# Second feed-forward of a two-layer block: down projection in fp32r halves, with the weight stationary

## The reference

```
def _L1_ffn_ref(x, Wr, Wg, Wu, Wd, Sg, Su, Sd):      # E, K, F = 16, 2, 64; FS = 128
    shared = silu(xf @ Sg) * (xf @ Su) @ Sd
    probs = softmax(xf @ Wr)
    topk_p, topk_i = top_k(probs, K)
    cw = zeros((T, 16)).at[arange(T)[:, None], topk_i].add(topk_p)
    for e in range(16):
        routed += (silu(xf @ Wg[e]) * (xf @ Wu[e]) @ Wd[e]) * cw[:, e:e+1]
    return routed + shared
```

## Time and profile before

| | |
|---|---|
| median of 3 runs | 1448.84 us (1448.66 to 1451.96) |
| the profiled execution | 1449.45 us, its span 1447.5 us |
| PE / PEld busy | 1299.0 / 988.7 us (90% / 68%) |
| DVE busy | 1126.0 us (78%) |
| ACT / POOL busy | 971.2 / 757.9 us (67% / 52%) |
| the second feed-forward | from about 1236 us to the end, some 211 us |
| its PE L2256 (down) | 576 matmuls and as many weight loads |

### The profile page before, as it was taken

How to read it: one execution, slowest core, us unless ns; L and a number is a source line. 1 busy time by engine, 2 the same in 40 slices (tenths; PEclk the granted TensorE clock), 3 DMA queues, 4 the chain that set the end, 5 groups by cost and what they waited for, 6 DMA issues and landing times. The chain is left out here.

```text
span 1447.5 us, 34194 instructions
## 1 busy us (share of the span) xinstructions
PE 1299.0 (90%) x12121; PEld 988.7 (68%) x12121; DVE 1126.0 (78%) x3042; ACT 971.2 (67%) x1499; POOL 757.9 (52%) x972
## 2 busy tenths in 40 slices
PE   2799999999999689999928999999999998799997
PEld 1466666666655377888816777777777776688886
DVE  5578888888877566999856888888888776476776
ACT  1688888888887357777724777777777877344441
POOL 4775675787763364899765454556444330101112
PEclk9899999999999779999957999999999999899999
DMA  6000000111111030222122111111111110225253
GB/s 237 18 22 22 20 22 21 25 30 34 29 31 40 8 89 28 60 74 74 56 84 55 49 48 48 47 48 47 49 47 38 40 41 19 58 61 128 71 132 82
DMA packets 84429, 77.20 MB, mean 53 GB/s; under 512 B 18224, under 2 KB 72240, under 8 KB 83888
## 3 DMA queue, kind: packets, MB, share of 16 engines
q1 hardware_dynamic: 80176, 66.73, 17.4%
q0 software_dynamic: 4096, 8.40, 2.0%
HBM read 36.26 MB, written 13.63 MB: 34 GB/s over the span
## 5 line engine op out<-in xcount | busy, mean ns | idle before, releaser
L541 ACT ACTIVATE a_p<-a_ps_s 128x1024 f32<-128x1024 f32 x256 | 258.4, 1031 | 21.6 <-PE a_ps_s L400 21.2
L1313 DVE TENSOR_REDUCE a_qt<-a_ps_d 128x2 fp32r<-128x512 f32 x256 | 174.9, 690 | 42.8 <-PE a_ps_d L1092 37.3
L651 DVE TENSOR_REDUCE a_qt<-a_ps_d 128x2 fp32r<-128x512 f32 x256 | 174.6, 688 | 40.1 <-PE a_ps_d L411 38.4
L822 POOL TENSOR_TENSOR a_rn<-a_ss,a_half 128x16 f32<-128x16 f32 x56 | 162.6, 2921 | 1.3
L1214 ACT ACTIVATE a_pg<-a_ps_s 128x1024 f32<-128x1024 f32 x128 | 125.8, 1024 | 24.0 <-PE a_ps_s L1081 22.4
L1092 PE MATMUL a_ps_d<-a_kpad,a_qs 128*128 128x512 f32 x256 | 126.4, 497 | 4.2 <-DVE a_qt L1313 1.5
L418 PE MATMUL a_ps_o<-a_p,a_v 128*32 128x256 f32 x2048 | 126.9, 387 | 3.7 <-ACT a_p L541 3.7
L411 PE MATMUL a_ps_d<-a_kpad,a_qs 128*128 128x512 f32 x256 | 126.2, 494 | 3.0 <-DVE a_qt L651 2.6
L2335 ACT ACTIVATE f_s<-f_ps_g 128x512 f32<-128x512 f32 x72 | 43.0, 598 | 99.5 <-PE f_ps_g L2271 99.3
L1501 POOL DMA_INDIRECT a_picked<-ys,rows x64 | 67.5, 1054 | 61.5 <-PE a_ps_d L1092 50.7
L418 PEld LDWEIGHTS a_ps_o<-a_p,a_v 128*32 128x32 f32 x2048 | 60.4, 110 | 51.3 <-issue 19.4
(11 more groups left out here) (370 smaller groups left out, 3829.7 us busy)
## 6 DMA issues: line engine op xcount, KB each, us to landing
a_kpad<-a_kc SPq DMA_DIRECT2D x512, 32.0 KB
f_gb<-spread SPq DMA_DIRECT2D x64, 256.0 KB, 5.6
a_kpad<-a_kq SPq DMA_DIRECT2D x256, 32.0 KB, 1.8
f_xin<-xs SPq DMA_DIRECT2D x39, 128.0 KB, 2.1
ys<-f_yout SPq DMA_DIRECT2D x39, 128.0 KB, 2.1
w<-in_w SPq DMA_DIRECT2D x2, 2304.0 KB, 11.5
out_x<-X SPq DMA_DIRECT2D x8, 256.0 KB, 6.6
xs<-f_zero SPq DMA_DIRECT2D x15, 128.0 KB, 1.9
```

The lines of the kernel that those rows point to most:

```text
L541: nc.scalar.activation(probs[:, u % 2, 2 * c:2 * c + 2, :, :].rearrange("p a b c -> p (a b c)"), ps_s[:, 2 * c:2 * c + 2, :].rearrange("p ...
L651: nc.vector.tensor_reduce(qt2[:, (k - PEAK) % 4, 2 * part:2 * part + 2, SHIFT], bank(k, f"m{part}")[:, :].rearrange("p (a b) -> p a b", b= ...
L822: nc.gpsimd.tensor_tensor(rn[:, part * c:(part + 1) * c], ss[:, part * c:(part + 1) * c], half[:, 0:c], ALU.pow).then_inc(rn_ready, 1)
L1313: nc.vector.tensor_reduce(qt[:, b % 2, GLOBAL, n:n + 2, SHIFT], bank(k, f"m{part}")[:, :].rearrange("p (j s) -> p j s", s=S), AX.X, ALU.ma ...
```

## The change

The down projection is done in fp32r halves, as the up projection already is. Per piece there are now three matmuls of 512 columns (weight high with product high, weight low with product high, weight high with product low), and the weight's halves wdh and wdl are stationary, so that the sum in ps_y has features on the partitions. The halves of the product are made anew for every piece: ACT casts it to ph (`high`), and POOL (q = 0, 2, 4, 6, 7, 8) or DVE (q = 1, 3, 5) subtracts ph from it into pl (`low`). ph and pl have three buffers each. The finished sum is copied to yb by ACT and turned back by four TensorE transposes into a new PSUM tile ps_b, from which DVE now takes statistics (at q = 3 and 4, before q = 1 and 2) and the normalisation. A piece of p is free when its pl is written (before: when `down` was done), and h[0] is free when pl of piece 0 is written. wdh and wdl are made once, in step 0.

```diff
+    BY_VECTOR = (1, 3, 5)
+    BY_POOL = tuple(q for q in range(NQ) if q not in BY_VECTOR)
+    TURN_BACK = 2
...
+        acc, yb = sb("acc", [P, TOK]), sb("yb", [P, TOK])
+        ph, pl = sb("ph", [P, 3, TOK], F32R), sb("pl", [P, 3, TOK], F32R)
+        wdh, wdl = sb("wdh", [P, NQ * D], F32R), sb("wdl", [P, NQ * D], F32R)
+        ps_b = pb("ps_b", [P, TOK])
...
@@ PE, down(st, q, block)
-                for t in range(TT):
-                    src = h[:, 0, t * P:(t + 1) * P] if q == 0 else p[:, q % 2, t * P:(t + 1) * P]
-                    last = nc.tensor.matmul(ps_y[:, t * D:(t + 1) * D], src, a["wd"][:, q * D:(q + 1) * D],
...
+                pe.wait_ge(ph_ready, st.at(lambda k: NQ * (k - block) + q + 1))
+                hi, lo = [w[:, q * D:(q + 1) * D] for w in (wdh, wdl)]
+                nc.tensor.matmul(ps_y[:, :], hi, ph[:, q % 3, :], start=q == 0, stop=False)
+                nc.tensor.matmul(ps_y[:, :], lo, ph[:, q % 3, :], start=False, stop=False)
+                pe.wait_ge(pl_by_vector if q in BY_VECTOR else pl_by_pool, st.at(lambda k: low_count(k - block, q)))
+                nc.tensor.matmul(ps_y[:, :], hi, pl[:, q % 3, :], start=False, stop=q == NQ - 1).then_inc(down_done, 1)
...
@@ PE, in the loop over q, behind down(st, q - 1, 1)
+                    if live(k - 2) and q == TURN_BACK:
+                        pe.wait_ge(y_copied, st.at(lambda k: k - 1))
+                        wait(pe, y_normed, st.at(lambda k: k - 2))
+                        for t in range(TT):
+                            last = nc.tensor.transpose(ps_b[:, t * P:(t + 1) * P], yb[:, t * P:(t + 1) * P],
+                                                       ident[:, :])
+                        last.then_inc(y_turned, 1)
...
@@ ACT
+            def high(st, q):
...
+                    act.wait_ge(p_ready, st.at(lambda k: gate_count(k, q)))
+                wait(act, down_done, st.at(lambda k: NQ * (k - 1) + q + 1 - 3))
+                src = h[:, 0, :] if q == 0 else p[:, q % 2, :]
+                nc.scalar.copy(ph[:, q % 3, :], src).then_inc(ph_ready, 1)
...
                     if q == 0 and live(k - 2):
...
-                        nc.scalar.copy(acc[:, :], ps_y[:, :]).then_inc(y_copied, 1)
+                        nc.scalar.copy(yb[:, :], ps_y[:, :]).then_inc(y_copied, 1)
+                    if live(k - 1):
+                        high(st, q)
...
+                    if k == 0 and q == 2:
+                        nc.scalar.copy(wdh[:, :], a["wd"][:, :]).then_inc(turned_copied, 1)
...
@@ DVE, by_gate(q) and what follows it
-                    wait(dve, down_done, st.at(lambda k: NQ * (k - 1) + q - 1 - (q == 1)))
+                    if q <= 2:
+                        wait(dve, pl_by_pool, st.at(lambda k: low_count(k - 2, q + 6) if k >= 2 else 0))
+                    else:
+                        dve.wait_ge(pl_by_vector if q - 2 in BY_VECTOR else pl_by_pool,
+                                    st.at(lambda k: low_count(k - 1, q - 2)))
...
+                def low(q):
+                    if not live(k - 1) or q not in BY_VECTOR:
+                        return
+                    dve.wait_ge(ph_ready, st.at(lambda k: NQ * (k - 1) + q + 1))
+                    nc.vector.tensor_tensor(pl[:, q % 3, :], p[:, q % 2, :], ph[:, q % 3, :].bitcast(F32),
+                                            ALU.subtract).then_inc(pl_by_vector, 1)
...
@@ hidden(q), q == 0
-                            dve.wait_ge(down_done, st.at(lambda k: NQ * (k - 1) + 1))
+                            dve.wait_ge(pl_by_pool, st.at(lambda k: low_count(k - 1, 0)))
...
                 for q in range(1, NQ):
                     by_gate(q)
+                    low(q - 1)
...
+                    if k == 0 and q == 8:
+                        dve.wait_ge(turned_copied, WD_HI)
+                        nc.vector.tensor_tensor(wdl[:, :], a["wd"][:, :], wdh[:, :].bitcast(F32), ALU.subtract
...
@@ POOL, ahead of and behind the power of the finished block
+                for q in (0, 2, 4):
+                    low(q)
...
+                for q in (6, 7, 8):
+                    low(q)
```

More of the change, by code:

```diff
@@ L2249, in down @@
                         pe.wait_ge(last_step, LAST_Y)
+                        pe.wait_ge(last_step, WD_LO)
                     wait(pe, y_copied, st.at(lambda k: k - block))
-                else:
-                    pe.wait_ge(p_ready, st.at(lambda k: gate_count(k + 1 - block, q)))
-                for t in range(TT):
-                    src = h[:, 0, t * P:(t + 1) * P] if q == 0 else p[:, q % 2, t * P:(t + 1) * P]
-                    last = nc.tensor.matmul(ps_y[:, t * D:(t + 1) * D], src, a["wd"][:, q * D:(q + 1) * D],
-                                            start=q == 0 and t == 0, stop=q == NQ - 1 and t == TT - 1,
-                                            skip_group_check=True)
-                last.then_inc(down_done, 1)
+                pe.wait_ge(ph_ready, st.at(lambda k: NQ * (k - block) + q + 1))
[4 more added lines that the diff above has]
+                nc.tensor.matmul(ps_y[:, :], hi, pl[:, q % 3, :], start=False, stop=q == NQ - 1).then_inc(down_done, 1)
             def up(st, q):
@@ L2275, in _ @@
                 last = nc.tensor.transpose(ps_y[:, t * P:(t + 1) * P], a["heads"][:, (B - 1) % 2, t, :], ident[:, :])
-            last.then_inc(turned_full, 1)
+            last.then_inc(last_full, 1)
             pe.wait_ge(rw_ready, 1)
@@ L2299, in _ @@
                                                     a["wo"][:, :], start=True, stop=True)
-                        last.then_inc(op_full, 1)
+                        last.then_inc(last_full, 1)
                     if live(k) and q == 6:
@@ L2452, in _ @@
                         last_batch(q)
-                    if q == 1 and live(k - 2):
-                        hold(dve, y_copied, st.at(lambda k: k - 1), passed)
+                    if k == 0 and q == 8:
+                        dve.wait_ge(turned_copied, WD_HI)
+                        nc.vector.tensor_tensor(wdl[:, :], a["wd"][:, :], wdh[:, :].bitcast(F32), ALU.subtract
+                                                ).then_inc(last_step, 1)
+                    if q == 3 and live(k - 2):
+                        hold(dve, y_turned, st.at(lambda k: k - 1), passed)
                         for t in range(TT):
-                            last = nc.vector.bn_stats(bn[:, t, :], acc[:, t * D:(t + 1) * D])
+                            last = nc.vector.bn_stats(bn[:, t, :], ps_b[:, t * D:(t + 1) * D])
                         last.then_inc(bn_done, 1)
-                    if q == 2 and live(k - 2):
+                    if q == 4 and live(k - 2):
                         hold(dve, bn_done, st.at(lambda k: k - 1), passed)
@@ L2464, in _ @@
                         dve.wait_ge(rs_ready, st.at(lambda k: k - 1))
[L2465 removed]
+                        wait(dve, x_new, st.at(lambda k: k - 2))
+                        normalise_tiles(nc, ps_b, mv, rs, acc).then_inc(y_normed, 1)
                     if not live(k):
@@ L2490, in _, with low @@
                     for n in range(2):
-                        pool.wait_ge(stats_last, n + 1)
+                        pool.wait_ge(last_step, (LAST_Y_STATS, LAST_X_STATS)[n])
                         nc.gpsimd.tensor_scalar(ve_last[:, :], mv_last[:, :, 1], EPS, None, ALU.add
-                                                ).then_inc(ve_last_ready, 1)
-                        pool.wait_ge(ve_last_ready, n + 1)
+                                                ).then_inc(pool_last, 1)
+                        pool.wait_ge(pool_last, LAST_VE[n])
                         nc.gpsimd.tensor_tensor(rs_last[:, :], ve_last[:, :], half[:, 0:TPB], ALU.pow
-                                                ).then_inc(rs_last_ready, 1)
+                                                ).then_inc(pool_last, 1)
                     pool.wait_ge(last_step, LAST_Z)
+                def low(q):
+                    if not live(st.k - 1):
+                        return
+                    pool.wait_ge(ph_ready, st.at(lambda k: NQ * (k - 1) + q + 1))
+                    src = h[:, 0, :] if q == 0 else p[:, q % 2, :]
+                    nc.gpsimd.tensor_tensor(pl[:, q % 3, :], src, ph[:, q % 3, :].bitcast(F32), ALU.subtract
+                                            ).then_inc(pl_by_pool, 1)
+                for q in (0, 2, 4):
+                    low(q)
                 if live(st.k - 2):
```

35 lines of the change are left out of this document (22 added, 13 removed).

## The result

| | before | after |
|---|---|---|
| median of the runs | 1449.88 us (1448.66 to 1451.96) | 1499.43 us (1498.74 to 1499.59) |
| ratio, 95% interval | | 1.0339 (1.0321 to 1.0357) |
| span of the profiled execution | 1447.5 us | 1496.9 us |

The account below looks back on a forecast made before the run. PE bounds, with DVE nearly as critical, so PE's gain counted as zero. Five steady steps at +5.0 us plus the first and last steps sum to 40.2 us on the profiled 1449.45, a median of 1489 us, range 1466 to 1516.

Parts of the forecast that it names:

- What bounds: Steady step: PE busy 23.61 of 23.95 us, DVE nearly as critical; PE's gain of 1.45 us a block counted as zero.
- Start: Logits to hidden(0): wait for down(0) replaced by an equal one for POOL, 5.45 us against 5.48; no gain.
- A: Steady step's start: two more ACT casts ahead of the exponential delay silu(2) and hidden(2); +0.5 us.
- B: Steady step: bn_stats on DVE moves from ahead of the wait for hidden(2) to behind it, at q = 3; +0.85 us.
- C: Steady step: DVE waits for POOL's subtracts at multiply of ex (0.3), small two-input chain (0.8), product 7 (0.75); +1.85 us.
- D: Steady step: DVE's own subtracts of products 3 and 5; +1.2 us.
- E: End of the step: logits wait for product 8's cast, POOL subtract and last matmul, 3.0 us behind its start; +0.75 us.
- Rival 2: PE's clock falls too at step starts, some 3 us each in six steps; 1507 us, chance 0.22.
- k = 7: Step 7: copy to gt stands behind cast(6), so the gates' DMAs and thus step 8 come 4.9 us later.
- k = 8: Step 8: eight products, three subtracts, statistics, normalisation and about three POOL waits of 1.1 on DVE, longer end; +5.3 us.
- Rival 1: POOL and DVE slip past each other, so their mutual waits are near nothing; step +3.1, 1475 us, chance 0.25.
- rival 3: Faster, PE decides: DVE's subtracts fall into its idle time, step 22.5 us; 1438 us, chance 0.07.

Follow-up runs that it names:

- e13: e12 without the third matmul of each product (two per product, products' low halves left out); ratio 1.0048 to before, step 24.04 us.
- e12: e10 with transposes back ahead of down(0) and bn_stats ahead of hidden(2); products' low halves left out; ratio 1.0042 to before, step 24.09 us.
- e5: Changed kernel with the turn-back transposes ahead of down(0) and bn_stats ahead of hidden(2), as before; ratio 1.0273 to before, step 28.29 us.
- e1: Changed kernel with POOL's six subtracts per block replaced by equally long memsets that read nothing (those low halves left out); ratio 1.0238 to before.
- e4: Changed kernel with the last down piece behind the next step's logits and ACT's cast of xh ahead of product 8's; ratio 1.0355 to before.
- e2: Changed kernel without any subtract, third matmul reading zeros without waiting (products' low halves left out), casts kept; ratio 1.0113 to before, step 25.60 us.
- e10: Changed kernel: DVE writes products 1 to 8 straight into ph, ACT casts piece 0 only, no subtracts, third matmul reads zeros; ratio 1.0048 to before.
- e3: Changed kernel with matmuls of zeros filling PE's holes at pieces 3, 5 and 8; ratio 1.0298 to before, step 29.36 us.
- after again: The changed kernel itself, unedited, measured again beside other experiments as their reference; 1499.48 us, ratio 1.0347 to before.

## Why the prediction was right

Forecast 1489 (1466 to 1516), result 1499.4: slower as forecast, by the mechanism named, and 10 us more. After's trace has the signs that were named for it: hidden(0) at 5.47 and released by POOL, product 7 at 1.53, PE idle for 0.62 ahead of the last matmul of piece 8. By the steps of the prediction:

- **What bounds.** "DVE is nearly as critical as PE" holds, and e13 makes it stronger: the chain through ACT's head and DVE's stretch gives 24.0 us, the step that before takes, with 2.85 us less of PE's work in it. Counting PE's gain as zero was right. Its size was 1.2 us at full clock (e12's 22.40 against 23.59) rather than 1.45.
- **Start, 0.** Right: hidden(0) at 5.47 and 5.46 behind the logits, against 5.48, released by POOL.
- **A, +0.5.** The head grew by 0.21 only.
- **B, +0.85.** bn_stats took 0.89 in the stretch; e5 gave 1.04 back, e12 only 0.58. Right.
- **C, +1.85.** Right in kind and place, at all three, too small: 0.64 + 0.93 + 0.84 = 2.4, of which e1 gets 1.6 back as time. The multiply of ex had been priced at 0.3.
- **D, +1.2.** Right: e1 less e2 in DVE's busy time in the stretch, 1.11.
- **E, +0.75.** From product 8's start to the logits it took 3.16 instead of 2.23, +0.93: 0.47 of it behind the start of xl, the rest in the stretch, mostly the 0.36 that xl now waits for xh. e4 shows that this could not be had back by itself.
- **Left out:** normalise now reads ps_b in PSUM instead of acc in SBUF: 1.36 against 1.11, +0.25, in the steady steps of every run with the new form.
- **Sum.** The terms add up to 5.82, and the step grew by 0.21 + 4.70 + 0.47 = 5.38 at full clock: the new work fills some 0.4 of DVE's short waits, where the prediction had taken off 0.15. That 5.0 was so near is in part luck: C and E too small and normalise left out, against A too large and more waits filled. By removal, one after the other: lock 1.60 (e1), subtracts 2.13 (e2), casts 0.93 (e10), order of bn_stats 0.58 (e12), rest 0.15: 5.39.
- **Rival 2, the clock,** came true beside the forecast, in three of the five steady steps and at the head of step 7, and at a smaller price: 1.3 us a fall rather than 3. The 3 us were read from before's step 1, where the clock stood at 0.50 for 6.8 us; after's falls at the head last 3.4. The double ones of e13 did cost 3. k = 2 to 6 became +4.7, +5.4, +6.6, +6.5 and +7.0, 30.3 in all against 25; 4.0 of these 5.3 us are falls (the heads of steps 4, 5 and 6, and 0.65 of stretch in step 6). The error was to treat the clock as an alternative instead of adding its share. With the 1.2 us of step 7 it is about 5 of the 10 us by which the forecast fell short by the traces; in the timed runs e3 gets 4 to 6 back.
- **The ends.** k = 0: +1.2 (1.3 forecast). k = 1: +1.6 (3). k = 7: +7.1 (4.9), where gt was copied 6.1 later. In after again, whose step 7 has no fall at its head, it was copied 4.9 later, as forecast, so 1.2 are the fall's; the last 1.0 lie behind gt, where the DMA to `spread` landed 2.9 us behind its issue in after, 1.5 in before and 1.5 in e3, for no reason that the runs show. k = 8: +7.8 (5.3), since DVE's products are held in five places:

```profile
1469.21 2.27 DVE L2454 TENSOR_TENSOR f_p<-f_h,f_gb 128x512 f32<-128x512 f32 x2 [3.21 <-DMA f_gb<-spread]
...
1472.35 1.68 DVE L2454 TENSOR_TENSOR f_p<-f_h,f_gb 128x512 f32<-128x512 f32 x1
...
1476.41 2.34 DVE L2454 TENSOR_TENSOR f_p<-f_h,f_gb 128x512 f32<-128x512 f32 x2
...
1479.63 1.82 DVE L2454 TENSOR_TENSOR f_p<-f_h,f_gb 128x512 f32<-128x512 f32 x1
...
1482.65 1.35 DVE L2454 TENSOR_TENSOR f_p<-f_h,f_gb 128x512 f32<-128x512 f32 x1
```

  Alone two products take 1.28 and one 0.69; here 4.8 us are waits, where the prediction had three of 1.1. k = 9: +1.4 (0.7). Sum of all 49.4.
- **Rival 1** (no lock) is refuted by e1; **rival 3** (PE decides) by e12 and e13.
- **Readings of the prediction that do not come out.** Of the X add beside a product, 0.53 us went by until the product ended and 1.12 followed, not 0.4 and 1.26; it took 0.39 more than alone, so that it waited still holds. The copy to yb was put at 0.50, where the earlier trace rows has copies of 0.57 and 0.58; it took 0.58. Neither moves the forecast.

What stays open: why the clock falls in some of the steps of one kernel and not in others that look the same (after's step 3 beside step 4), and the 1.7 us that separate e2 from before are only split by order of removal, which another order would split differently.

## What to carry to other kernels

Where an engine at 98% busy is followed closely by another, take the second one's chain as the bound before you pay for relieving the first: here nine matmuls fewer a step bought nothing (e13 against e12). Find the stretch in which the following engine hardly waits and add up only what lands in it; the longest hole of the busy engine may be the place where it waits and not what it costs. Beside a GpSimd instruction that reads SBUF, every VectorE instruction with two SBUF inputs that starts inside it is to be counted as waiting for its end (26 of 26 here).

## What the runs showed of the hardware

- A fall of the clock needs no long hole of PE. In e10 it fell at 1337.6, and the holes in the 13 us before were 0.65, 0.75, 0.27 and 0.52 us:

```profile
1335.50:1337.50 2.00, 2.00 (x15) 1.91 (x16) 0.42 (x2) 0.00 (x0) 0.16 (x1) 1.00 1.05 231
1337.50:1338.50 1.00, 1.00 (x5) 0.76 (x4) 0.92 (x3) 0.56 (x2) 0.00 (x0) 0.57 1.08 236
1338.50:1340.50 2.00, 2.00 (x6) 1.61 (x5) 0.69 (x1) 1.03 (x3) 0.00 (x0) 0.50 1.08 229
```

  The Trainium skill, "TensorE: Matmul & The Clock Gate", section "HAM oscillation — how this bites in real kernels", gives as the rule that PE must have no long idle gap; here only short ones came before a fall, so in this case that rule does not suffice.
- POOL's memset and VectorE's two-input product ran side by side at full speed (e1), POOL's subtract and that product did not: the product ended 0.55 us behind the subtract's end, nearly its whole 0.69.
- Four VectorE tensor_scalar of 128 columns in a row took 1.36 us with their input in PSUM and 1.11 with it in SBUF; one by itself is 0.40 and 0.34 long.
